# Cross attention of a decoder layer on one core: the next batch's row statistics tile by tile during the attention, and its input turned between the last outputs

## The reference

```python
x = x + _L0_xattn_ref(_layernorm(x, axis=-1), ctx, ctx, mask, W_q, b_q, W_k, b_k, W_v, b_v, W_o, b_o)

def _layernorm(x, axis=-1, eps=1e-05):
    m = jnp.mean(x, axis=axis, keepdims=True)
    v = jnp.var(x, axis=axis, keepdims=True)
    return (x - m) / jnp.sqrt(v + eps)

Q = (q @ W_q.T + b_q)          # from the normalized x; 4 batches, 1024 rows, 16 heads of 32
K = (k @ W_k.T + b_k)          # K and V from ctx
V = (v @ W_v.T + b_v)
scores = Q K^T / sqrt(32), causal and padding mask
out = softmax(scores) V
return out @ W_o.T + b_o
```

## Time and profile before

| | |
|---|---|
| runs (3) | median 4476.57 us, 4475.96 to 4482.53 |
| profiled execution | 4481.21 us, its span 4479.5 |
| busy in the span | PE 4064.1 (91%), DVE 3152.3 (70%), ACT 1652.2 (37%), POOL 1034.0 (23%) |
| cross attention | from about 2240 to 3530 us of the span |
| turns of a batch | outputs start at 2548.05, 2865.60 and 3181.86 us |

### The profile page before, as it was taken

One profiled execution on the slowest core, in us unless ns is written; L12 is line 12 of the kernel. 1 busy time (PEld: TensorE's weight loads), 2 busy tenths in 40 slices (PEclk: granted clock), 3 DMA queues, 4 the chain that ended last, 5 costly groups with the idle time before them and its releaser, 6 DMA issues. The chain is left out here.

```text
span 4479.5 us, 71612 instructions
## 1 busy us (share of the span) xinstructions
PE 4064.1 (91%) x26200; PEld 3023.7 (68%) x26200; DVE 3152.3 (70%) x6457; ACT 1652.2 (37%) x3472; POOL 1034.0 (23%) x597
## 2 busy tenths in 40 slices
PE   6999999998799999999778888898898799999999
PEld 5767676765566666666466676576576478787877
DVE  5787878774489999899657647657557566666664
ACT  3434343432333333343237537447357311111111
POOL 0333434343055555555500000000000000000000
PEclk8999999999899999999889999999999899999999
DMA  2110111001201111111143142242341310101000
GB/s 107 37 37 29 38 42 39 28 35 39 86 26 51 44 39 45 51 44 37 40 175 100 62 142 84 92 134 62 117 126 50 121 34 24 34 22 36 27 26 19
DMA packets 150049, 266.40 MB, mean 59 GB/s; under 512 B 30276, under 2 KB 36424, under 8 KB 149704
## 3 DMA queue, kind: packets, MB, share of 16 engines
q1 hardware_dynamic: 149704, 261.83, 17.5%
HBM read 164.88 MB, written 88.34 MB: 57 GB/s over the span
## 5 line engine op out<-in xcount | busy, mean ns | idle before, releaser
L1866 DVE TENSOR_REDUCE xa_mn<-xa_s 128x1 f32<-128x896 f32 (+7 forms) x512 | 373.0, 751 | 135.8 <-PE xa_s L1961 134.8
L1781 ACT ACTIVATE xa_src<-xa_s,xa_mn 128x896 f32<-128x896 f32 (+7 forms) x512 | 377.7, 740 | 231.6 <-DVE xa_mn L1866 230.3
L1967 PE MATMUL xa_gen<-xa_ident,xa_src 128*128 128x128 f32 x2304 | 310.2, 278 | 53.3 <-ACT xa_pT L1790 26.3
L73 PE MATMUL ff_wb<-ff_w_hi,ff_st_hi 128*128 128x512 f32 x768 | 323.8, 422 | 10.4 <-DVE ff_parts L2472 10.4
L940 DVE SCALAR_TENSOR_TENSOR mb_cv<-mb_xc,mb_cw,mb_cv 128x256 f32<-128x256 f32 x432 | 310.8, 773 | 31.9 <-ACT mb_xc L746 27.8
L1728 POOL TENSOR_TENSOR xa_res<-xa_res,xa_bor 128x512 f32<-128x512 f32 x32 | 40.5, 1270 | 1244.7 <-DMA xa_res<-after_mamba_dram 1244.7
L74 PE MATMUL ff_wb<-ff_w_hi,ff_st_lo 128*128 128x512 f32 x768 | 311.9, 406 | 0.0
L75 PE MATMUL ff_wb<-ff_w_lo,ff_st_hi 128*128 128x512 f32 x768 | 311.1, 405 | 0.0
L1967 PEld LDWEIGHTS xa_gen<-xa_ident,xa_src 128*128 128x128 f32 x2304 | 251.1, 143 | 75.1 <-ACT xa_src L1781 59.5
L1309 PE MATMUL mb_ib<-mb_wc,mb_yT 128*128 128x512 f32 x512 | 262.6, 661 | 1.8 <-DVE mb_y L1078 1.0
L2240 POOL TENSOR_TENSOR ff_mixed<-ff_at,ff_rw 128x1024 f32<-128x1024 f32 x32 | 60.9, 1904 | 875.3 <-DVE ff_at L2500 875.3
(11 more groups left out here) (494 smaller groups left out, 11031.7 us busy)
## 6 DMA issues: line engine op xcount, KB each, us to landing
xa_qa<-xa_q_dram SPq DMA_DIRECT2D x384, 64.0 KB, 2.0
xa_q_dram<-xa_kq SPq DMA_DIRECT2D x32, 512.0 KB, 2.8
xa_k_dram<-xa_kq SPq DMA_DIRECT2D x32, 512.0 KB, 2.8
xa_ka<-xa_k_dram SPq DMA_DIRECT2D x192, 64.0 KB, 2.0
xa_st<-xa_k_dram SPq DMA_DIRECT2D x192, 64.0 KB, 2.0
mf_xg<-in_x_dram SPq DMA_DIRECT2D x16, 512.0 KB, 5.1
turned_dram<-mf_xt_hi SPq DMA_DIRECT2D x16, 512.0 KB, 2.7
turned_dram<-mf_xt_lo SPq DMA_DIRECT2D x16, 512.0 KB, 4.0
```

The lines of the kernel that those rows point to most:

```text
L73: nc.tensor.matmul(out, w_hi, x_hi, start=first, stop=False)
L1781: a_.activation(pq[:, hh, 0:w], s1[g, i, hh][:, 0:w], ACT.Exp, scale=-1.0, bias=mn[:, i % 2, hh:hh + 1], accum_out=sums[:, i // QT, i % QT ...
L1866: v_.tensor_reduce(mn[:, i % 2, hh:hh + 1], s1[g, i, hh][:, 0:(i + 1) * P], AX.X, ALU.min).then_inc(mx_ready.sem, 1)
L1967: last = tr(ps[:, n * P:(n + 1) * P], pq[:, hh, j * P:(j + 1) * P], ident[:])
```

## The change

- **Statistics ahead.** For batches 1 to 3 the tiles of x are loaded one by one into the two halves of `res` (`peek`, SP, new) while the attention of the batch before runs in groups 1 and 2, when `res` is free. `stats` reads `res` there and is issued at the end of a tile of the attention: tile t's at the end of attention tile t + 10, counted from 0. The loads of tiles 0 and 1 are issued at the end of attention tile 9, that of tile t + 2 at the end of the one that holds `stats` t, after it.
- **The chain in pieces.** The 24 steps of the two chains follow three at a time at the ends of the next eight attention tiles (`ln_step`).
- **The turn.** The head's statistics and chains are gone from it. x is loaded into `src` as before, normalized after `o` 3 (tiles 0 to 3) and after the splits 0 and 1 (tiles 4 to 7); the `source` steps 0 to 3 are put between the outputs 4, 5 and 6. Steps 4 to 7 stay in the body.
- Batch 0 keeps its head.

The core of the diff:

```diff
+        def ahead(g, i):
+            n = g * NT + i - NT - 1
+            if n == 0:
+                yield "peek", 0
+                yield "peek", 1
+            if 1 <= n <= NT:
+                yield "stats", n - 1
+                if n + 1 < NT:
+                    yield "peek", n + 1
+            if NT < n <= 2 * NT:
+                for _ in range(LN_STEPS):
+                    yield "ln_step", (n - NT - 1) // QT
...
                 if now and now[0] == NHG - 1 and now[1] > QT + 1:
                     yield "o", now[1] - QT - 2
+                if now:
+                    yield "ahead", now
...
+                    if it > 0 and what == "src" and n < AHEAD_SRC:
+                        continue
...
                 yield "load_mask", it + 1, 0
+                for t in range(QT):
+                    yield "xn", it + 1, t
                 yield "o", it, QT
-                ahead = [n for n in head() if n[0] != "load_x"]
-                cut, end = ahead.index(("xn", 0)), ahead.index(("ln", 1)) + 1
-                for what, n in ahead[:cut]:
-                    yield what, it + 1, n
+                yield "src", it + 1, 0
+                yield "src", it + 1, 1
+                for t in range(QT, NT):
+                    yield "xn", it + 1, t
                 yield "o", it, QT + 1
-                for what, n in ahead[cut:end]:
-                    yield what, it + 1, n
+                yield "src", it + 1, 2
+                yield "src", it + 1, 3
+                yield "mask", it + 1, 0
                 yield "o", it, QT + 2
-                for what, n in ahead[end:]:
-                    yield what, it + 1, n
                 yield "o", it, QT + 3
...
                     if t == 0:
+                        if it + 1 < B:
+                            sp.wait_ge(stat_ready.sem, stat_ready.at(it + 1, NT - 1))
                         load_res(0)
...
+                def peek(t):
+                    sp.wait_ge(o_moved[t % 2].sem, o_moved[t % 2].at(it - 1, 0))
+                    if t >= 2:
+                        sp.wait_ge(stat_ready.sem, stat_ready.at(it, t - 2))
+                    sp.dma_start(res[:, t % 2, :], x_in[it, t * P:(t + 1) * P, :]).then_inc(peek_loaded[t % 2].sem, 16)
...
                 def stats(t):
-                    dve.wait_ge(x_loaded[t // 4].sem, x_loaded[t // 4].at(it, 0))
+                    if it:
+                        dve.wait_ge(peek_loaded[t % 2].sem, peek_loaded[t % 2].at(it - 1, t // 2))
+                    else:
+                        dve.wait_ge(x_loaded[t // 4].sem, x_loaded[t // 4].at(it, 0))
                     if t == 0:
                         dve.wait_ge(xn_ready.sem, xn_ready.at(it, -1))
-                    last = v_.bn_stats(stat[:, t, :], src[:, t, :])
-                    if t % QT == QT - 1:
-                        step(last)
+                    x = res[:, t % 2, :] if it else src[:, t, :]
+                    v_.bn_stats(stat[:, t, :], x).then_inc(stat_ready.sem, 1)
...
                 def normed(t):
+                    dve.wait_ge(x_loaded[t // 4].sem, x_loaded[t // 4].at(it, 0))
```

More of the change, by code:

```diff
@@ L110, in rsqrt, with rsqrt_steps @@
         step(nc.vector.scalar_tensor_tensor(out, a, 1.5, out, ALU.add, ALU.mult))
+def rsqrt_steps(nc, step, out, x, v, a, scale, eps):
+    step(nc.vector.tensor_scalar(v, x, scale, eps, ALU.mult, ALU.add))
+    yield
+    step(nc.vector.tensor_scalar(out.bitcast(I32), v.bitcast(I32), -0.5, RSQRT_SEED, ALU.mult, ALU.add))
+    yield
+    for _ in range(3):
+        step(nc.vector.tensor_tensor(a, out, out, ALU.mult))
+        yield
+        step(nc.vector.scalar_tensor_tensor(a, a, -0.5, v, ALU.mult, ALU.mult))
+        yield
+        step(nc.vector.scalar_tensor_tensor(out, a, 1.5, out, ALU.add, ALU.mult))
+        yield
 def split_weight(nc, dve, stage, stage_loaded, hi_ready, half_ready, n, hi, lo):
@@ L1470, in cross_attention @@
         stored = [sig(f"stored{i}", NT // 2, 16) for i in range(2)]
-        dve_step = sig("dve_step", 2 * (2 + RSQRT_STEPS))
+        peek_loaded = [sig(f"peek_loaded{i}", NT // 2, 16) for i in range(2)]
+        stat_ready = sig("stat_ready", NT)
+        dve_step = sig("dve_step", 2 * (1 + RSQRT_STEPS))
         const_ready, par_loaded, const_dve = sem("const_ready"), sem("par_loaded"), sem("const_dve")
@@ L1572, in order @@
                 for what, n in body():
+                    if what == "ahead":
+                        if it + 1 < B:
+                            for what, n in ahead(*n):
+                                yield what, it + 1, n
+                        continue
+                    if it > 0 and what == "src" and n < AHEAD_SRC:
+                        continue
                     if it == 0 and what == "load_ctx":
@@ L1705, in output @@
                     sp.dma_start(out[it, t * P:(t + 1) * P, :], res[:, t % 2, :]).then_inc(stored[t % 2].sem, 16)
-                return {"fetch": fetch, "load_mask": mask, "load_x": load_x, "load_ctx": load_ctx, "kq": store, "load": load, "scale": move,
+                def peek(t):
[3 more added lines that the diff above has]
+                    sp.dma_start(res[:, t % 2, :], x_in[it, t * P:(t + 1) * P, :]).then_inc(peek_loaded[t % 2].sem, 16)
+                return {"peek": peek, "fetch": fetch, "load_mask": mask, "load_x": load_x, "load_ctx": load_ctx, "kq": store, "load": load, "scale": move,
                      "o": output}
@@ L1843, in norm_x, with norm_step @@
                     step(last)
-                    rsqrt(nc, step, xr[:, mine], mv[:, mine, 1], tmp[:, 0, mine], tmp[:, 1, mine], 1.0, EPS)
+                    yield
+                    yield from rsqrt_steps(nc, step, xr[:, mine], mv[:, mine, 1], tmp[:, 0, mine], tmp[:, 1, mine], 1.0, EPS)
+                def norm_x(half):
+                    for _ in norm_steps(half):
+                        pass
+                chains = {}
+                def norm_step(half):
+                    if half not in chains:
+                        chains[half] = norm_steps(half)
+                    next(chains[half])
                 def normed(t):
+                    dve.wait_ge(x_loaded[t // 4].sem, x_loaded[t // 4].at(it, 0))
                     x = src[:, t, :]
```

12 lines of the change are left out of this document (8 added, 4 removed).

## The result

The changed kernel takes **4561.14 us** (median of 4 runs, 4557.95 to 4563.29), the kernel before in the same frame 4478.88. The ratio is 1.0186, with a 95% interval of 1.0173 to 1.0198: slower by 82 us, where 4554 (4518 to 4585) was forecast. Its profiled execution has a span of 4557.9 at a mean granted clock of 0.954, the one before 4479.5 at 0.961.

The account below looks back on a forecast made before the run. Attention bound by three engines handing over tiles, turns by VectorE. Stalls 34.6 + 42.9, statistics 3.7, run-ahead -6, clock 9, uncovered work 3 make 87 slower; less 10.4 at turns, 77: 4554 us median, range 4518 to 4585.

Parts of the forecast that it names:

- The two stalls: Attention, each batch made ahead: VectorE waits for x's loads before statistics 0 and 7; 34.6 and 42.9 us in all.
- Around the stalls: Attention: statistics after stalls 3.7, VectorE waits falling away -6, lower TensorE clock 9, uncovered VectorE work 3 us.
- Statistics behind stalls: Attention, VectorE: the statistic itself runs after each of six stalls, 6 x 0.62 = 3.7 us.
- uncovered work: Attention, VectorE: added statistics and chain steps not hidden in its waits, 1 us per batch, 3 in all.
- The clock: Attention: TensorE leaves idle stretches at the lower clock, 1.5 us per stall, 9 in all.
- the run-ahead: Attention: TensorE continues with the next tile during stalls, so VectorE's own waits fall away; 6 us saved, at most 17.
- The turn: Between batches: second projection starts 37.8 us after the outputs' start; gains 3.9, 1.8 and 4.7, together 10.4.
- Rival 1: Attention stalls do not come, only turns gain: 4466 us, or 4456 with the round trip hidden; chance 0.06.
- Rival 3: Attention stalls come, turns gain nothing, more clock loss: 4570 us, or 4582 with VectorE's work half uncovered; chance 0.10.
- Rival 2: Attention stalls come but more is repaid, no clock loss, turns' round trip hidden: about 4520 us; chance 0.12.
- Rival 4: Whole kernel: the change does nothing measurable, the turns giving back some 29 us each; chance 0.02.
- The Trainium skill: SP's queue: DMA start time is "usually small relative to the DMA itself"; by that the stalls would go, giving rival 1's time.

Follow-up runs that it names:

- Experiment 2: Changed kernel, with the load of x's eighth tile issued on SP ahead of group 3's 48 loads instead of behind them: 4512.47 us, ratio to before 1.0078.
- experiment 3: Changed kernel, with x's loads ahead and the moves of the heads' outputs issued from GpSimd's queue instead of SP's: 4471.36 us, ratio to before 0.9991.
- experiment 4: Changed kernel, queues kept, with x's loads ahead, statistics and chain steps shifted later, to where SP has no string: 4483.50 us, ratio to before 1.0010.
- Experiment 1: Changed kernel, with only x's eight loads ahead issued from GpSimd's queue instead of SP's: 4506.92 us, ratio to before 1.0072.
- experiment 5: On top of experiment 3, statistics of batches 1 to 3 over 8 columns instead of 512 and no chain steps: 4462.72 us, ratio to before 0.9968.
- Experiment 9: Changed kernel, with the first projection of batches 1 to 3 computed twice to fill TensorE's wait: 4551.45 us, ratio to before 1.0169.

## Why the prediction was right, point by point

- **The two stalls: right.** 77.5 forecast, 74.7 measured: first 11.93, 10.99 and 10.35 for 10.4, 12.1 and 12.1; second 13.44, 14.49 and 13.52 for 13.7, 14.9 and 14.3. Where a load stands on its queue, when the queue reaches it, and when the consumer wants it, were enough. Experiments 2 to 4 take one stall of a batch or both away in three ways, and each time the loss goes with them.
- **Its cause: right, and incomplete.** I named the 48 loads and the move as standing ahead of tile 0's load. Experiment 1 shows that the move holds a second load by its buffer: on a free queue tile 1's load still waited 26.34 for it. In the changed kernel tile 1's statistic, at 2410.08, does not wait: the stall at tile 0 has held VectorE as well.
- **Around the stalls: right in sum, not in parts.** Statistics behind stalls 3.7 and uncovered work 3 make 6.7; experiments 3 and 5 give 1.4, 3.4 and 2.4, together 7.2. Without stalls I had expected 3 of it (experiment 5), so VectorE's slack hid less than I thought. The clock less the run-ahead, 9 - 6 = 3, is 2.9, 1.8 and 1.4, together 6. 87 was forecast for the attention and 87 came; that it fits so well is luck, since the stalls were forecast 2.8 too high and the clock 3 too low.
- **The turn: its mechanism right, its gain mis-sized, 10.4 forecast and 5.8 measured.** The steps hold: transposes wait for output 3's sum (1.03 for 1.3), the first split comes at the last output, output 7's round trip takes 6.97 (from its store at 2600.05 to its sum's end at 2607.02) for 6.9, the second projection comes at 37.0 for 37.8. But I measured the gain at that projection's *first* matmul and took it as kept. TensorE waits 3.62, 1.85 and 3.53 ahead of it and runs all or most of it at the low clock, so 7 of 12.8 are lost again. Experiment 9 fills the wait and keeps 12.5 (47.35 - 42.73, 45.18 - 42.76 and 48.13 - 42.69). I had charged that clock to the stalls and not to the new wait at the turn. This is the term of the sum that was mis-sized.
- **The rivals.** Rival 1, no stalls, would have given 4466; experiments 3 and 4 build that case, and it is 4471 and 4484. Rival 3, in which the turn gains nothing (4570), lies 9 above the measured time, the forecast 7 below it. So the time alone hardly decides between them; the parts do, and they lie between: the turn gained half of what I forecast, and the clock cost more. Rivals 2 and 4 did not come.
- **The Trainium skill.** The sentence weighed in the prediction ("DMA: Bandwidth & Descriptors", "Issuing engines are not separate DMA queues") holds for one load, 0.45 to issue against 2.0 to land. Its "usually small" does not hold for a string: 48 took 25.1 of SP again, and giving the loads and moves another queue was worth 90 us (4561 to 4471), of which 8 came at the turns.

The attention and the turns make 87 - 5.8 = 81 of the 82 measured; the other 1 lies within what repeated runs of one kernel differ by.

## What to carry to other kernels

A prefetch is as early as its place in its issuing queue: look for the strings ahead of it, and for what must leave its buffer, and on which queue that stands. The cheapest mend may be a different moment on the same queue (experiments 2 and 4). At a turn, measure a gain after the next full-length work, not at its first instruction: a new idle stretch of TensorE can be paid again at the lower clock, as it was in 15 of 18 turns here.

## What was not expected

- Useless work made the turns shorter: 12 matmuls more at each of three turns, 2.8 us each, took 6.6 us off them. The granted clock over the second projection was 1.00, where it had been 0.50 after 3.62 of idling.
- The turn of experiment 3 is shorter than the changed kernel's (fourth projection at 41.12, 42.90 and 43.02) though only DMAs changed queue. VectorE's sum of output 3 starts 7.24 after the outputs' start (2555.38 - 2548.14), in the changed kernel 10.40 (2582.79 - 2572.39). There the load of its residual stood on SP behind the last move and half of x (issued 2573.96, 2574.47, 2575.16); in experiment 3 the move is not on SP, and that load went out at 2545.05, before the outputs. That this is the cause was not tried by itself, and it can only be part: the second projection comes 1.2 to 1.7 earlier (35.39, 35.65 and 35.76), and the rest goes with where the low clock falls. Experiment 2, whose turn is the changed kernel's, has its fourth projections at 42.96, 45.42 and 43.77.
- 256 KB loads into `res` land 3.3 after their issue from GpSimd's queue, 2.7 from SP's; neither the issue (0.54 of GpSimd) nor the 0.6 shows in the time of experiment 5's attention.
